# The head of a fused attention and mixture-of-experts block rebuilt: gate rows, row order, PSUM banks and the first turn's order

## The reference

```python
x = L0_attn_x                                   # (8, 512, 128)
mod = (_silu(L0_c) @ L0_wmod).reshape(8, 6, 1, -1)
sa, ca, ga, sb, cb, gb = (mod[:, i] for i in range(6))
ga = (2 * (ga >= 0) - 1) * jnp.maximum(jnp.abs(ga), 0.25)     # gb likewise
h = _layernorm(x) * (1 + ca) + sa
x = x + ga * attn(h)      # 16 heads of 8, causal softmax, Wo, layernorm * gamma + beta
h = _layernorm(x) * (1 + cb) + sb
x = x + gb * ffn(h)       # shared expert and the top 2 of 8 experts of width 64
```

## Time and profile before

| what | us |
|---|---|
| median of 3 runs | 563.61 |
| lowest and highest run | 563.37, 567.88 |
| the profiled execution's own time | 562.72 |
| its span (first to last instruction) | 561.0 |
| head, to the first score matmul | 34.07 |
| first turn | 52.0 |
| a regular turn | 60.5 |

### The profile page before, as it was taken

One profiled execution on the slowest core, in us unless ns is written; L12 is line 12 of the kernel. 1 busy time (PEld: TensorE's weight loads), 2 busy tenths in 40 slices (PEclk: granted clock), 3 DMA queues, 4 the chain that ended last, 5 costly groups with the idle time before them and its releaser, 6 DMA issues.

```text
span 561.0 us, 10206 instructions
## 1 busy us (share of the span) xinstructions
PE 501.3 (89%) x3628; PEld 273.6 (49%) x3643; DVE 375.2 (67%) x813; ACT 291.1 (52%) x614; POOL 256.5 (46%) x363
## 2 busy tenths in 40 slices
PE   1657989999999999999999999999999998999386
PEld 1433444554655464556555465546455644554144
DVE  6368986688567757775768756775777476861244
ACT  1103555766467546756575646664675546564220
POOL 6135427724664357625672466435752534244100
PEclk9977799999999999999999999999999999997669
DMA  5264412411432113410342144212341031001000
GB/s 124 73 180 103 128 44 82 156 46 43 100 115 85 45 51 93 157 44 17 88 158 52 34 99 133 68 44 58 88 156 43 2 103 24 3 0 39 0 2 19
DMA packets 46931, 40.66 MB, mean 72 GB/s; under 512 B 8088, under 2 KB 42656, under 8 KB 46880
## 3 DMA queue, kind: packets, MB, share of 16 engines
q1 hardware_dynamic: 39232, 36.92, 23.5%
q10 hardware_dynamic: 7648, 3.09, 2.1%
HBM read 24.91 MB, written 14.68 MB: 71 GB/s over the span
## 4 chain that ended last, share of the span: by engine, by line
PE 65%; DVE 16%; ACT 7%; issue 2%; DMA 1%; POOL 1%; DVEq 0%; POOLq 0%
PE s_bank L1018 10%; PE pv_bank L1047 10%; PE s_bank L1033 8%; PE gate_bank L1100 7%; DVE row_max L856 7%; PE up_bank L1111 6%; PE gate_bank L1133 6%; PE s_bank L1020 4%; PE misc L976 3%; PE misc L998 3%; ACT probs L659 3%; DVE stats_x L799 2%; PE up_bank L1071 2%; ACT square L685 2%; PE misc L1081 1%
## 5 line engine op out<-in xcount | busy, mean ns | idle before, releaser
L856 DVE TENSOR_REDUCE row_max<-s_bank 128x1 f32<-128x512 f32 (+3 forms) x352 | 212.2, 636 | 38.9 <-PE s_bank L1020 35.9
L659 ACT ACTIVATE probs<-s_bank 128x512 f32<-128x512 f32 x320 | 181.4, 597 | 65.3 <-PE s_bank L1033 60.7
L1018 PE MATMUL s_bank<-k_stack,q_stack 72*128 72x256 bf16 (+3 forms) x512 | 133.0, 308 | 13.0 <-DVE row_max L856 6.9
L1033 PE MATMUL s_bank<-q_stack,k_stack 75*128 75x128 bf16 (+3 forms) x512 | 116.9, 305 | 8.2 <-ACT probs L659 6.9
L559 POOL TENSOR_SCALAR_AFFINE_SELECT probs<-probs 128x512 f32<-128x512 f32 (+1 forms) x96 | 76.6, 804 | 88.4 <-ACT probs L659 87.8
L1020 PE MATMUL s_bank<-causal,ident_bf 128*128 128x128 bf16 x512 | 98.9, 223 | 0.0
L1047 PE MATMUL pv_bank<-probs,v_aug 128*32 128x512 f32 (+3 forms) x1024 | 91.4, 454 | 0.4 <-POOL probs L559 0.3
L1018 PEld LDWEIGHTS s_bank<-k_stack,q_stack 72*128 72x128 bf16 x512 | 50.6, 99 | 66.9 <-DVE row_max L856 48.6
L1033 PEld LDWEIGHTS s_bank<-q_stack,k_stack 75*128 75x128 bf16 x512 | 41.7, 98 | 55.5 <-ACT probs L659 25.6
L1020 PEld LDWEIGHTS s_bank<-causal,ident_bf 128*128 128x128 bf16 x512 | 51.0, 100 | 15.2 <-issue 6.2
L544 POOL TENSOR_TENSOR hidden<-hidden,coef_sb 128x512 f32<-128x512 f32 x28 | 35.6, 1273 | 22.1 <-ACT coef_sb L704 22.1
(11 more groups left out here) (150 smaller groups left out, 587.3 us busy)
## 6 DMA issues: line engine op xcount, KB each, us to landing
q_stack<-q_scr SPq DMA_DIRECT2D x96, 96.0 KB
k_stack<-k_scr SPq DMA_DIRECT2D x96, 96.0 KB
k_scr<-k_parts SPq DMA_DIRECT2D x14, 256.0 KB, 2.5
q_scr<-q_parts SPq DMA_DIRECT2D x7, 384.0 KB, 2.3
k_scr<-k_parts SPq DMA_DIRECT2D x7, 384.0 KB, 2.4
x_res<-in_L_attn_x SPq DMA_DIRECT2D x8, 256.0 KB, 3.9
out_x<-out_sb SPq DMA_DIRECT2D x8, 256.0 KB, 2.6
x_in<-in_L_attn_x ACTq DMA_DIRECT2D x7, 256.0 KB, 2.6
```

What stands on the lines that cost most here:

```text
L659: nc.scalar.activation(dst, src, ACT.Exp, scale=SCALE).then_inc(exp_done, 1)
L856: nc.vector.reduce_max(row_max[s % 2][:, 0, h:h + nh, qt], s1_bank[u % 2][:, 0:nh * w].rearrange("p (h k) -> p h k", h=nh), AX_X).then_inc ...
L1018: nc.tensor.matmul(dst[:, w * i:w * (i + 1)], q_stack[0:KROWS, h, P * qt:P * (qt + 1)], k_stack[0:KROWS, h, 0:w], start=True, stop=False)
L1033: final = nc.tensor.matmul(dst[:, at:at + w], k_stack[0:MROWS, hh, P * j:P * (j + 1)], q_stack[0:MROWS, hh, P * j:T], start=True, stop=True)
```

## The change

- **Gates on 8 partitions.** `spread` and the 16 matmuls go. Two matmuls with the condition as weights give both gates as rows of batches, [8, 256], in `gate_bank`; DVE forms the gates and multiplies gamma and beta there with seven instructions on 8 partitions, at the end of the head. ACT writes the [8, 3, 128] result to DRAM (`mod_scr`), and one transfer spreads it over 128 partitions as `mods` [128, 8, 3, 128], 12 KB a partition. The tasks `mod0` to `mod4` go.
- **Row order.** The columns of Wq and Wk are reordered on ACT (two copies), so that within a group of four heads the rows go by dimension and then head; the biases come in that order by four small transfers each. `q_scr` is now [3, 128, 512] and `k_scr` [5, 128, 512], its slots holding the parts 0, 1, 2, 0, 1, so that a rotation is a window of three slots. k is written with two transfers instead of five, and `stack_rows` loads (part, d) rows as 24 pieces of 4 KB instead of 96 of 1 KB, again six transfers a group.
- **Banks.** In the head k goes to `s2_bank[0]` and v to `s2_bank[1]`; k is made before q. Part 1 of both is made by ACT. ACT writes and loads the q rows of group 0, SP the k rows.
- **Start.** x comes in two halves, SP issues all input loads except bk, tanh does not wait for wmod, x_n goes ahead of the shift and scale columns, and POOL clears one `v_aug` before and one after x_n.
- **Order of the turns.** The tables become `ORDER` with entries "first", "middle", "final" and "tail". "first" is new; the other three hold the old tables without the dropped tasks. `centre0` moves from the third stage of the first turn to its first, `centre1` from the third to the fourth.

The diff, cut to its core:

```diff
+ORDER = {
+    "first": {
+        "extra": [
+            {0: [("xin", "next")], 3: [("xs", "next")], 10: [("o", "")], 16: [("xn", "next"), ("centre0", "first")],
...
+             27: [("msplit", "cur")], 28: [("mods", "first")], 29: [("xt", "next")], 31: [("max", "cur")],
+             33: [("uev", "")]},
...
+            {2: [("q", "next")], 5: [("k", "next")], 6: [("o", "")], 19: [("msplit", "cur")],
+             20: [("stack", "next")], 22: [("uev", "")], 29: [("max", "cur")]},
+            {5: [("v", "next")], 9: [("uev", "")], 20: [("o", "")], 28: [("max", "cur")], 30: [("msplit", "cur")]},
+            {13: [("uev", "")], 23: [("centre1", "first")], 25: [("msplit", "cur")], 29: [("max", "cur"), ("o", "")]},
...
+        "s1": [[0, 1, 2, 9, 11, 11, 15, 16, 22, 25, 29],
+               [0, 1, 2, 3, 4, 11, 14, 16, 22, 23, 24],
+               [0, 5, 8, 8, 8, 9, 10, 12, 15, 18, 19],
+               [0, 0, 1, 2, 3, 6, 7, 7, 8, 12, 18]],
+        "s2": [[0, 0, 0, 0, 0, 0, 1, 1, 1, 4],
+               [3, 3, 8, 10, 12, 20, 23, 26, 28, 29],
+               [8, 9, 11, 13, 16, 16, 22, 23, 28, 29],
+               [2, 3, 4, 5, 6, 7, 9, 11, 17, 28]],
+        "pv": [[14, 14, 19, 26],
+               [23, 1, 12, 24],
+               [23, 7, 7, 15],
...
-    "xin", "xs", "cond", "xn", "late", "xt", "q", "spread", "k", "stack", "v", "gates0", "gates1", "gates2", "gates3")]
+    "xin", "xs", "cond", "xn", "cols", "late", "xt", "k", "q", "stack", "v", "gates")]
...
-    q_scr = nc.dram_tensor("q_scr", [P, PARTS, T], BF16, kind="Internal").ap()
-    k_scr = [nc.dram_tensor(f"k_scr{r}", [P, PARTS, T], BF16, kind="Internal").ap()
-             for r in range(PARTS)]
+    q_scr = nc.dram_tensor("q_scr", [PARTS, P, T], BF16, kind="Internal").ap()
+    k_scr = nc.dram_tensor("k_scr", [K_SLOTS, P, T], BF16, kind="Internal").ap()
+    mod_scr = nc.dram_tensor("mod_scr", [B, 3, C], F32, kind="Internal").ap()
...
+        def stack_rows(eng, stack, scr, at, r, g):
+
+            eng.dma_start(stack[SROWS * r:SROWS * (r + 1), GH * g:GH * (g + 1), :],
+                          scr[at:at + PARTS, GROUP * g:GROUP * (g + 1), :].rearrange("s (d h) t -> s d (h t)", h=GH)
+                          ).then_inc(stacked[g], 16)
+
+        def bias_column(eng, col, row):
+            for g in range(G):
+                rows = slice(GROUP * g, GROUP * (g + 1))
+                eng.dma_start(col[rows, :], row[rows].rearrange("(h d) -> d h", h=GH),
+                              allow_slow_non_contiguous=True).then_inc(qkv_in, 16)
+
+        def write_q(eng, rows, done):
+            eng.dma_start(q_scr[:, rows, :].rearrange("s p t -> p s t"), q_parts[rows, :, :]).then_inc(done, 16)
+
+        def write_k(eng, rows, done):
+            eng.dma_start(k_scr[0:PARTS, rows, :].rearrange("s p t -> p s t"), k_parts[rows, :, :]).then_inc(done, 16)
+            eng.dma_start(k_scr[PARTS:K_SLOTS, rows, :].rearrange("s p t -> p s t"),
+                          k_parts[rows, 0:PARTS - 1, :]).then_inc(done, 16)
...
-            sp.dma_start(x_in[:, :, :], tok(x, 0)).then_inc(x_in_ready, 16)
+            for i in range(2):
+                tiles = slice(TT // 2 * i, TT // 2 * (i + 1))
+                sp.dma_start(x_in[:, tiles, :], tok(x, 0)[:, tiles, :]).then_inc(x_half_in[i], 16)
             sp.dma_start(cond_sb[:, :], cond).then_inc(cond_in, 16)
-            sp.dma_start(wmod_sb[:, :], wmod).then_inc(cond_in, 16)
-            for dst, src in ((wq, Wq), (wk, Wk), (wv, Wv)):
+            sp.dma_start(wmod_sb[:, :], wmod).then_inc(wmod_in, 16)
+            for dst, src in ((wq_in, Wq), (wk_in, Wk), (wv, Wv)):
...
+            def load_stacks(it, g):
 
                 need(sp, s2_written, it * (G * U2) + U2 * (g + 1 - G))
-                need(sp, written, it * (16 * SCR_DMAS) + 16 * SCR_DMAS)
-                heads = slice(GH * g, GH * g + GH)
+                need(sp, scr_written, it * (16 * SCR_DMAS) + 16 * SCR_DMAS)
                 for r in range(PARTS):
-                    rows = slice(SROWS * r, SROWS * (r + 1))
-                    for stack, scr in ((q_stack, q_scr), (k_stack, k_scr[r])):
-                        src = scr.rearrange("(h d) s t -> (d s) h t", d=DH)
-                        sp.dma_start(stack[rows, heads, :], src[:, heads, :]).then_inc(stacked[g], 16)
+                    stack_rows(sp, q_stack, q_scr, 0, r, g)
+                    stack_rows(sp, k_stack, k_scr, r, r, g)
...
+                    if first(it):
+                        sp.wait_ge(k_split, 1)
+                        write_k(sp, slice(0, GROUP), k_first_written)
+                        sp.wait_ge(minus_ones, 1)
+                        sp.wait_ge(k_first_written, 32)
+                        for r in range(PARTS):
+                            stack_rows(sp, k_stack, k_scr, r, r, 0)
+                        sp.wait_ge(q_split, 1)
+                        write_q(sp, slice(GROUP, P), scr_written)
+                        write_k(sp, slice(GROUP, P), scr_written)
+                        load_stacks(0, 1)
+                    else:
                         sp.wait_ge(q_split, it + 2)
-                        sp.dma_start(q_scr[rows], q_parts[rows]).then_inc(done, 16)
+                        write_q(sp, slice(0, P), scr_written)
                         sp.wait_ge(k_split, it + 2)
-                        sp.dma_start(k_scr[0][rows], k_parts[rows]).then_inc(done, 16)
-                        for r in range(1, PARTS):
-                            sp.dma_start(k_scr[r][rows, 0:PARTS - r, :], k_parts[rows, r:PARTS, :]).then_inc(done, 16)
-                            sp.dma_start(k_scr[r][rows, PARTS - r:PARTS, :], k_parts[rows, 0:r, :]).then_inc(done, 16)
-                        if done is first_written:
-                            sp.wait_ge(minus_ones, 1)
-                            load_stacks(0, 0, first_written)
-                    if isinstance(it, int) and it < 0:
-                        load_stacks(0, 1)
+                        write_k(sp, slice(0, P), scr_written)
...
+            nc.gpsimd.memset(v_aug[0][:, :, :, :], 0.0)
 
             def late_constants():
+                pool.wait_ge(x_norm, 1)
+                nc.gpsimd.memset(v_aug[1][:, :, :, :], 0.0).then_inc(const_step, 1)
...
+            bias_column(act, bk_col, bk)
+            act.wait_ge(cond_in, 16)
             nc.scalar.activation(cond_t[:, :], cond_sb[:, :], ACT.Tanh, scale=0.5).then_inc(ct_step, 1)
...
+            for dst, src in ((wq, wq_in), (wk, wk_in)):
+                final = nc.scalar.activation(dst[:, :].rearrange("c (g d h) -> c g d h", g=G, d=DH),
+                                             src[:, :].rearrange("c (g h d) -> c g d h", g=G, h=GH), ACT.Copy)
+            final.then_inc(qk_ordered, 1)
...
+            def first_batch(src, made, col, parts, rest, at_first, read, n, second):
+
+                act.wait_ge(made, n)
+                nc.scalar.activation(parts[:, 0, :], src[:, :], ACT.Identity, bias=col[:, 0:1]).then_inc(at_first, 1)
+                act.wait_ge(read, n)
+                nc.scalar.activation(parts[:, 1, :], rest[:, :], ACT.Copy).then_inc(second, 1)
...
+                    act.wait_ge(q_split, 1)
+                    write_q(act, slice(0, GROUP), q_first_written)
+                    act.wait_ge(q_first_written, 16)
+                    for r in range(PARTS):
+                        stack_rows(act, q_stack, q_scr, 0, r, 0)
...
+                if name == "gates" and first(it):
+
+                    act.wait_ge(rows_made, 1)
+                    act.dma_start(mod_scr, mod_rows[:, :, :]).then_inc(rows_written, 16)
+                if name == "mods":
+                    act.wait_ge(rows_written, 16)
+                    act.dma_start(mods[:, :, :, :].rearrange("p b i c -> p (b i c)"),
+                                  mod_scr.rearrange("b i c -> (b i c)").unsqueeze(0).to_broadcast([P, B * 3 * C])
+                                  ).then_inc(mods_in, 16)
...
-            def gates(i):
-
-                dve.wait_ge(cond_mm, 3 + i)
-                gate, banks = ((gate_a, s1_bank), (gate_b, s2_bank))[i // 2]
-                half = B // 2
-                nc.vector.tensor_copy(gate[:, half * (i % 2):half * (i % 2 + 1), :],
-                                      banks[i % 2][:, 0:half * C].rearrange("p (b c) -> p b c", b=half)).then_inc(gates_read, 1)
...
-            def modulation(i):
-
-                gate, at = (gate_a, gate_b)[i // 2 % 2], 6 + 4 * (i // 2)
-                if i == 0:
-                    dve.wait_ge(gates_read, 4)
-                if i < 4:
-                    dve.wait_ge(ct_step, 6 + 2 * i)
-                if i in (0, 2):
-                    nc.vector.tensor_scalar(gate_sign[:, :, :], gate[:, :, :], 0.0, 2.0, ALU.is_ge, ALU.mult).then_inc(ct_step, 1)
...
+            def gates():
+
+                dve.wait_ge(cond_mm, 3)
+                raw = gate_bank[0:B, 0:2 * C].rearrange("b (i c) -> b i c", i=2)
```

(43 more changed lines are left out.)

267 lines of the change are left out of this document (146 added, 121 removed), and 85 rows, old and new, of tables (LATER, ORDER, S1_STEPS, S2_STEPS).

## The result

The changed kernel is slower: 573.39 us, median of 4 runs (571.12 to 577.93), where the kernel before had 564.71 on the same chip (4 runs, 563.37 to 567.88). The ratio is 1.0143, 95% interval 1.0097 to 1.0189. Forecast was 563.6 us, no change. The profiled execution took 577.93 (span 575.8, mean granted clock 0.929) where the one before took 562.72 (span 561.0, clock 0.957), so the traces stand 15 us apart and the medians 9: the profile caught the slowest of the four.

The account below looks back on a forecast made before the run. PE is busy 58.63 of 60.49 us in regular turns, so only the first turn's start (2.0 us earlier) and length counted, summing to 0.0; 562.72 + 0.0 + 0.9 for the median gave 563.6 us, range 549 to 577.

Parts of the forecast that it names:

- Part 1: Head up to h1T: x_n stall goes, k_stack memset stands still 1.8 us; h1T at 12.2, 3.0 us earlier.
- the rival's 10.9: Head: the k_stack memset, which starts first, might lose nothing to POOL's memset, and h1T come at 10.9 us.
- Part 2: Projections in the head: k goes first, in its own bank; k ready at 17.8 us, q at 20.0.
- Part 3: Head's stack transfers: loads on three engines, 72 GB/s, 8.2 us a group; first turn starts at 32.0, 2.0 us earlier.
- Part 4: First turn: matmuls with the maxima 6.0 us later, dropped work gives time back; end at 86.0, where it was 86.03.
- the rest of the second stage: First turn, from the first matmul needing the maxima to the third stage: 8.8 us, where it was 13.85.
- time outside both is taken as unchanged: Only the first turn's start and its length are counted; everything outside these two numbers stays as before.
- The planned order of its own I value at nothing beyond this: First turn's new order of work: no gain beyond the terms already counted, bounds -3 and +3 us.
- Part 5: Regular turns: fewer k writes, nothing waits for them; SP's wait for last loads covered by 1.5 us, cost 0.
- B: Stack loads: three engines at the maxima's 17 GB/s each, 11.6 us a group, regular turns slower too; 585 us, chance 0.20.
- A: Stack loads spread over 12 or more engines: first turn starts at 26.5, maxima there at 41.6; 550.0 us, chance 0.20.
- C: Three engines, first turn gains: memset free (-1.8), broadcast misses loads (-4.2), order gives 2; 555.6 us, chance below 558 0.13.

Follow-up runs that it names:

- delayed kernel: The kernel with eight-engine loads and the maxima ahead of the third group's loads, plus an extra half-length memset ahead of the k_stack memset: 555.68 us.
- both repairs: Changed kernel with the loads' dimension of eight outermost (eight engines) and the first maxima issued on SP ahead of the third group's loads: 552.86 us, ratio 0.979.

## Why the prediction was wrong

**Part 1, right in direction, one term too high.** h1T came at 10.53, not 12.2. I let DVE's k_stack memset stand still for 1.8 us while POOL cleared v_aug; the rows show both at their own length, 3.47 and 1.80. That is near the rival's 10.9, which I took from the Trainium skill, SBUF — State Buffer, section "SBUF: two separate sides" (who starts first loses nothing). But its reason isn't what happened: POOL's memset started second and lost nothing either, so these two did not exclude each other at all. The x_n stall went, 1.11 us for four.

**Part 2, right.** k's write was issued at 16.49 (17.8 forecast), which is most of part 1's lead.

**Part 3, right.** Three engines, 71 to 77 GB/s (72 forecast), a group's time 7.8 us (8.2): groups 2 and 3 and the maxima land from 44.20 to 59.79. The first score came at 30.45 (32.0 forecast).

**Part 4, wrong: the step "Group 2, issued ahead of the first maxima on SP's queue, takes 8.2 more, and the maxima's small transfer stands behind it".** It counted one group too few. In the new tables the first stage's `max` has step 31, and a stage has 30 steps, so on SP it sorts behind the next stage's `load`, which is group 3. The changed kernel's 59.84 is 44.24 plus two groups of 7.8; I had 47.0 plus one, 55.2; the 47.0 was itself 2.8 too late, mostly by the collision with the spread of the gates (4.2 forecast, 1.7 by the move of that transfer), which hid part of the missing group. With the maxima two steps earlier on SP, they are in at 52.4.

**Part 4, mis-sized: the rest of the second stage, 8.8 us.** It took 12.9 at a clock of 0.50 and 10.2 at 0.79. I added 0.25 for a colder PE, though my own forecast left PE idle for many microseconds just ahead of this stretch, which in the traces goes with the low level: by these two stretches the price was 2.7. The third stage, forecast 10.0, took 12.1, partly at clock 0.88; the fourth, forecast 12.0, took 11.1. So the first turn ended at 96.0, not 86.0: 4.6 us by the maxima (59.84 for 55.2), 4.1 by the rest, 2.1 and -0.9 by the last two stages.

**Part 4, outside my count: "time outside both is taken as unchanged".** centre1 moved to the end of the first turn, and the first stage of the next one rose by 4.9 us. The delayed kernel divides such a rise, 4.3 us with both repairs, into 1.4 of order and 2.8 of clock. By the copies the trace's difference is 10.8 at copy 4, 4.9 here, 0.4 up to out_sb and -1.3 behind it, 14.8 together.

**Part 4, out of its bounds: "The planned order of its own I value at nothing beyond this: bounds -3 and +3 us".** With eight engines and the maxima ahead, the new tables, the spread's place included, were worth 5.4 us at out_sb and 8.0 in the medians. With three engines no run separates this term.

**Part 5, right.** Full turns are 60.5 us in all traces; SP's longest wait for the last loads is 7.7 us and nothing waits for SP:

```profile
SPq L322 <- DMA k_stack<-k_scr: 49.0, 8, 7.7
```

**Rivals.** B, the slower side, gave the right sign by the wrong mechanism: neither slower engines nor late regular turns. A, twelve engines, was false as a reading of the change, but its number, 550.0, describes the repair, 552.9: first score at 26.5 and maxima used at 41.6 by its terms, 26.57 and 42.27 in the trace. That the totals come so near is in part luck, since the next turn's first stage then loses 4.3 us and the end of the program gives back 3.8 (414.5 to 410.7). C had a part: the memset cost the head nothing and the order gained, but the broadcast cost 1.7, not 4.2, and the missing group hid it all.

## What to carry to other kernels

Before pricing a small, urgent transfer, write out everything that its queue issues ahead of it, stage borders included; a step number beyond a stage's length puts it behind the next stage's loads. Read for each transfer how many DMA engines its outer dimension allows, and put the dimension that divides well outermost: here one reordered pattern was worth 12 us of 573. Where a profile stands within 1% of its rival, compare event by event, because stretches of low clock move by several microseconds when nothing but the start of the program does. When an experiment puts an old table back, list everything that stands in it: here the table held an order and a repair, whose effects nearly cancelled. And before warming an engine over a wait, see whether that engine or a transfer ends the stage.

## What the hardware showed that I had not expected

- A load in the new form keeps its issuing queue busy for 0.68 us on three engines and 0.64 on eight, where the old form took 0.31 to 0.38. Eighteen of them occupy SP for 13.5 us (32.24 to 45.7).
- The engine count follows the outermost dimension also at 8 (3 before the reorder), with the same 4 KB pieces. The Trainium skill, DMA: Bandwidth & Descriptors, section "Why a DMA increments its semaphore by 16 and not by 1", says so, and the packet counts agree. With eight engines SP takes 4.2 us to issue a group's six loads (55.74 to 59.92), and the DMA share is 0.42 in 57:60, where eight busy engines would show 0.50. That fits a pace set by the issue and not by the data; no run tests it.
- A delay of 2.25 us at the start made one stage 2.8 us shorter, clock 1.00 instead of 0.70 and 0.73, with the same work and the same DVE-bound stretch ahead of it. What decides where the clock falls was not settled here.
- In the last turn the same code ran at 1.00 or 0.69 for 15 us and so cost 0 or about 4 us, in different kernels and in different runs of one kernel.
